# Layer 0's prologue in a new order: block 0's x loaded second, constants on two queues, the statistics of the other blocks inside block 0, the attention weight products spread out

## The reference, cut to what matters

```
xn = layernorm(x)
x  = x + mamba_block(xn) + moe(xn)          # layer 0
xn = layernorm(x)
x  = x + latent_attention(xn) + top2_moe(xn) # layer 1

mamba_block(x): r = rmsnorm(x) * rms_w
    xi, z = split(r @ in_proj)               # 256 + 256
    xi = silu(causal_conv4(xi) + conv_b)
    dt, B, C = split(xi @ x_proj)            # 8 + 16 + 16
    delta = softplus(dt @ dt_w + dt_b);  A = -exp(A_log)
    h = exp(delta*A) * h + (delta*xi)*B      # a scan over 256 tokens, 256 x 16 states
    return x + ((h . C) + xi*D) * silu(z) @ out_proj
moe(x): softmax over 8 experts, top-p 0.8 gate, 8 experts 128 -> 512 -> 128 with relu
```

## Time and profile before

| | |
|---|---|
| device time, median of 3 runs | 2266.21 us (2262.88 to 2268.63) |
| the profiled execution: device time, span | 2265.14 us, 2263.3 us |
| busy in the span | PE 1996.5 us (88%), DVE 1732.8 (77%), ACT 1335.6 (59%), POOL 1288.6 (57%) |
| granted TensorE clock, mean | 0.942 |
| layer 0's prologue (to the first scan) | 100.64 us |
| layer 0 / layer 1 boundary | near 1480 us |

### The profile page before, as it was taken

The page is one execution under the profiler, slowest core; times in us unless marked ns, Lnnn a source line. Parts: engine busy times, 40 slices in busy tenths (PEclk is TensorE's granted clock), DMA queues, the critical chain, the costliest instruction groups (busy, mean ns, idle before and its releaser), DMA issues. The chain is left out here.

```text
span 2263.3 us, 40460 instructions
## 1 busy us (share of the span) xinstructions
PE 1996.5 (88%) x13648; PEld 1155.7 (51%) x13714; DVE 1732.8 (77%) x2781; ACT 1335.6 (59%) x2421; POOL 1288.6 (57%) x972
## 2 busy tenths in 40 slices
PE   1799999999999999999999999945899999998885
PEld 0455555555555555555555555533455555544442
DVE  3498888888888889888888888854777777765544
ACT  1576776776776776766767767611355555544442
POOL 0477867767767767767768777623322222224540
PEclk9999999999999999999999999955899999998987
DMA  7514505415325335335145055041222222233437
GB/s 192 136 41 107 130 27 127 112 39 128 97 51 132 86 67 132 76 77 132 53 99 131 30 118 122 15 123 63 83 92 87 88 88 88 88 112 102 141 94 227
DMA packets 197004, 222.49 MB, mean 98 GB/s; under 512 B 28872, under 2 KB 139504, under 8 KB 192688
## 3 DMA queue, kind: packets, MB, share of 16 engines
q1 hardware_dynamic: 194736, 215.52, 37.0%
q0 software_dynamic: 2048, 4.18, 0.7%
HBM read 165.41 MB, written 54.27 MB: 97 GB/s over the span
## 5 line engine op out<-in xcount | busy, mean ns | idle before, releaser
L685 POOL TENSOR_TENSOR dBx<-REP,BC 128x1024 f32<-128x1024 f32 x256 | 603.0, 2358 | 288.2 <-DVE dA L845 243.2
L845 DVE TENSOR_TENSOR_SCAN dA<-dA,dBx 128x512 f32<-128x512 f32 x512 | 626.6, 1224 | 115.1 <-ACT dA L555 66.2
L374 PE MATMUL UP<-xnT,W 128*128 128x512 f32 x1024 | 518.4, 626 | 52.0 <-ACT hT L564 40.1
L383 PEld LDWEIGHTS DN<-W,hT 128*128 128x128 f32 x4096 | 469.4, 192 | 109.3 <-issue 97.6
L383 PE MATMUL DN<-W,hT 128*128 128x128 f32 x4096 | 496.0, 278 | 0.3 <-ACT GD L571 0.3
L564 ACT ACTIVATE hT<-UP,b 128x512 f32<-128x512 f32 x512 | 355.1, 694 | 88.7 <-PE UP L374 85.0
L555 ACT ACTIVATE dA<-REP,A 128x512 f32<-128x512 f32 x512 | 354.1, 695 | 72.4 <-DVE PR L854 72.1
L854 DVE TENSOR_TENSOR PR<-dA,BC 128x512 f32<-128x512 f32 x512 | 353.6, 691 | 31.5 <-DVE dA L845 18.8
L1705 DVE TENSOR_REDUCE NM<-S 128x4 f32<-128x1024 f32 (+1 forms) x192 | 234.5, 1221 | 148.5 <-PE S L1264 93.5
L374 PEld LDWEIGHTS UP<-xnT,W 128*128 128x128 f32 x1024 | 180.6, 195 | 278.5 <-issue 146.2
L1466 ACT ACTIVATE PT<-S 128x1024 f32<-128x1024 f32 x192 | 196.4, 1023 | 181.5 <-PE S L1278 135.2
(11 more groups left out here) (246 smaller groups left out, 2809.6 us busy)
## 6 DMA issues: line engine op xcount, KB each, us to landing
REP<-s_delta SPq DMA_DIRECT2D x128, 256.0 KB, 7.8
REP<-s_dx SPq DMA_DIRECT2D x128, 256.0 KB, 7.3
BC<-s_b SPq DMA_DIRECT2D x128, 256.0 KB, 8.7
s_parts<-SPL SPq DMA_DIRECT2D x32, 384.0 KB, 2.8
s_dx<-tz SPq DMA_DIRECT2D x16, 512.0 KB, 3.1
s_y<-zeros SPq DMA_DIRECT2D x32, 256.0 KB, 4.8
WE<-in_L_ffn_we SPq DMA_DIRECT2D x32, 256.0 KB, 4.5
YC<-s_y SPq DMA_DIRECT2D x16, 512.0 KB, 4.9
```

Source lines behind the costliest of these rows:

```text
L374: nc.tensor.matmul(UP[k % 2][:], W1[:, e % E0, f * P:(f + 1) * P], xnT[:, q, :], start=True, stop=True).then_inc(upf.sem, 1)
L383: last = nc.tensor.matmul(DN[:, j * P:(j + 1) * P], hT[:, e % 2, f, j * P:(j + 1) * P], W2[:, e, f, :], start=(f == 0), stop=(f == FB - 1))
L685: nc.gpsimd.tensor_tensor(dBx[:, s % 2], DX[:, h, j:j + 2, :], BC[:, q // 2, q % 2, :].unsqueeze(1).to_broadcast([P, 2, T0]), ALU.mult).th ...
L845: nc.vector.tensor_tensor_scan(h, h, dBx[:, k // 2 % 2, k % 2, :], 0.0, ALU.mult, ALU.add).then_inc(scan_done.sem, 1)
```

## The change

The first load takes eight tiles, the tiles of blocks 0 and 1, and their `norms` run at once (`FIRST` = 8 tiles, `OTHERS` = 56, in 7 DMAs of 8). SP then loads `XI` of block 0, five constants (`first_loads`, semaphore `needed`), ten constants (A_log, `xproj`; semaphore `loaded`), `dloads`, the other tiles of x, `wloads`, `forget`, b2. ACT issues the nine other constants itself. `prep` hangs on `needed` alone; scaling `outproj` and A moves to s = 4 (`prep2`). The `norms` of the other tiles are cut in three parts that run on DVE in slots 8, 12 and 15 of block 0, with their square roots on ACT in slots 9 and 13; the first user is now block 2. The weight products stand at s = 0, 2, 8, 9, 12. `start()` on all engines moves from h = 31 to h = 27. `BC<-s_b` of the first half (4 DMAs) goes out right after the store of B and C.

```diff
-    XC, XT = 6, (NT - J0) // 6
+    XC, XT = 7, (NT - 2 * J0) // 7
...
-    FIRST, OTHERS = slice(0, J0), slice(J0, NT)
-    STATS_END = 2 * XC
-    PROJ0 = 8
+    FIRST, OTHERS = slice(0, 2 * J0), slice(2 * J0, NT)
+    STATS_AT = {2: (0,), 4: (1,), 5: (2,), 6: (3,), 7: (4,), 8: (5, 6)}
+    LAST_STATS = 8
+    NORMS_AT, ROOTS_AT = (8, 12, 15), (9, 13)
+    PE_PROJ = {0: ((0, 0),), 2: ((0, 1), (1, 0)), 8: ((1, 1),), 9: ((2, 0),), 12: ((2, 1),)}
+    ACT_PROJ = {1: ((0, 0),), 3: ((0, 1),), 4: ((1, 0),), 9: ((1, 1), (2, 0)), 13: ((2, 1),)}
+    PREP_AT = 4
+    START_AT = 27
...
+            if h == START_AT:
+                start()
             if h >= HS - EARLY:
                 fore(h - HS, 1, 1)
-        start()
...
             if h == -EARLY and start:
                 load_x(0)
+                for dst, src in first_loads:
+                    sp.dma_start(dst, src, allow_slow_non_contiguous=True).then_inc(needed, 16)
+                for dst, src in loads[:10]:
+                    sp.dma_start(dst, src, allow_slow_non_contiguous=True).then_inc(loaded, 16)
+                sp.wait_ge(zeroed, 1)
+                for dst, src in dloads:
+                    sp.dma_start(dst, src, allow_slow_non_contiguous=True).then_inc(dloaded, 16)
+                for g in range(XC):
+                    tiles = slice(2 * J0 + g * XT, 2 * J0 + (g + 1) * XT)
+                    sp.dma_start(X0[:, tiles, :], xd[:, tiles, :]).then_inc(xloaded[g + 1], 16)
                 for dst, src in wloads:
                     sp.dma_start(dst, src, allow_slow_non_contiguous=True).then_inc(wloaded, 16)
-                for dst, src in dloads:
-                    sp.dma_start(dst, src, allow_slow_non_contiguous=True).then_inc(dloaded, 16)
+                for par in range(2):
+                    for k in range(HALF):
+                        sp.dma_start(seqs(d_d[par][k * P:(k + 1) * P, :])[:, :, 0:1], forget[:].unsqueeze(2), allow_slow_non_contiguous=True).then_inc(forgot, 16)
...
                 if start:
                     load_x(1)
+                    load_states(0, n, q)
...
-        pe.wait_ge(loaded, LOADED)
+        pe.wait_ge(needed, NEEDED)
         pe.wait_ge(prep, 1)
...
         def start():
+            pe.wait_ge(prep2, 1)
             pe.wait_ge(wloaded, 16 * (len(wloads) + J0))
...
+        for dst, src in loads[10:]:
+            act.dma_start(dst, src, allow_slow_non_contiguous=True).then_inc(loaded, 16)
...
+            if first and h in ROOTS_AT:
+                root(OTHERS, ROOTS_AT.index(h), stat_step2, root_done2)
...
-                if isinstance(n, int) and n == 1:
+                if isinstance(n, int) and n == 2:
                     pool.wait_ge(stat_step2, 21)
...
+            if first and h in NORMS_AT:
+                norms(OTHERS, NORMS_AT.index(h), stat_step2, root_done2)
```

More of the change, by code:

```diff
@@ L243, in _ @@
         xd = tokens(dram["L0_attn_x"].rearrange("b t d -> (b t) d"))
[L244 to L253, removed]
-                sp.dma_start(seqs(d_d[q][k * P:(k + 1) * P, :])[:, :, 0:1], forget[:].unsqueeze(2), allow_slow_non_contiguous=True).then_inc(forgot, 16)
         for s in (xi_loaded, b_stored, d_stored, e_stored, *bc_loaded, *dr_loaded, *dx_loaded, xo_stored):
             sp.sem_inc(s.sem, 2 * s.per)
+        sp.dma_start(X0[:, FIRST, :], xd[:, FIRST, :]).then_inc(xloaded[0], 16)
         def load_rep(rep, src, h, loaded):
@@ L334, in fore @@
                 load_dx(0, n, q)
-            elif h == SP_AT["bc0"]:
+            elif h == SP_AT["bc0"] and not start:
                 load_states(0, n, q)
@@ L452, in fore @@
             if h == PE_AT["xproj"]:
+                if isinstance(n, int) and n == 0:
+                    pe.wait_ge(loaded, LOADED)
                 pe.wait_ge(xi_done.sem, xi_done.at(n, 1))
@@ L495, in between @@
         def between(s):
-            if PROJ0 <= s < PROJ0 + 6:
-                project((s - PROJ0) // 2, (s - PROJ0) % 2)
+            for n, part in PE_PROJ.get(s, ()):
+                project(n, part)
         def end(it, par):
@@ L509, in _, with root @@
             act.sem_inc(s.sem, 2 * s.per)
-        def roots(tiles, stat_step, root_done):
-            act.wait_ge(stat_step, 7)
-            nc.scalar.activation(stats[:, tiles, 0], q1[:, tiles], ACT.Sqrt).then_inc(root_done, 1)
-            act.wait_ge(stat_step, 15)
-            nc.scalar.activation(stats[:, tiles, 0], q2[:, tiles], ACT.Sqrt).then_inc(root_done, 1)
-        roots(FIRST, stat_step, root_done)
-        act.wait_ge(loaded, LOADED)
-        nc.scalar.activation(A[:], A[:], ACT.Exp).then_inc(aexp, 1)
+        def root(tiles, part, stat_step, root_done):
+            act.wait_ge(stat_step, (7, 15)[part])
+            nc.scalar.activation(stats[:, tiles, 0], (q1, q2)[part][:, tiles], ACT.Sqrt).then_inc(root_done, 1)
+        for dst, src in loads[10:]:
+            act.dma_start(dst, src, allow_slow_non_contiguous=True).then_inc(loaded, 16)
+        for part in range(2):
+            root(FIRST, part, stat_step, root_done)
+        act.wait_ge(needed, NEEDED)
         act.wait_ge(prep, 1)
@@ L539, in between @@
         def between(s):
-            if PROJ0 <= s < PROJ0 + 6:
-                project((s - PROJ0) // 2, (s - PROJ0) % 2)
-            if s == STATS_END:
-                roots(OTHERS, stat_step2, root_done2)
+            for n, part in ACT_PROJ.get(s, ()):
+                project(n, part)
+            if s == PREP_AT:
+                act.wait_ge(loaded, LOADED)
+                nc.scalar.activation(A[:], A[:], ACT.Exp).then_inc(aexp, 1)
         LAST_IN_BANK = {0: -1, 1: 0, 2: -2}
@@ L577, in start @@
             act.wait_ge(wTc, 6)
+            act.wait_ge(prep2, 1)
             make_da(TILES, -1)
@@ L766, in fore @@
                 tri = tri8[:].rearrange("p (e o) -> p e o", o=E0).unsqueeze(1).to_broadcast([P, J0, E0, E0])
+                if isinstance(n, int) and n == 0:
+                    pool.wait_ge(loaded, LOADED)
                 pool.wait_ge(gate_step.sem, gate_step.at(n, 7))
@@ L820, in between @@
                     last = nc.vector.bn_stats(stats[:, i, :], X0[:, i, :])
-                if s == STATS_END - 1:
-                    last.then_inc(stat_step2, 1)
-            elif s == STATS_END:
-                norms(OTHERS, stat_step2, root_done2)
-            elif s == SLOTS - 1:
+            if s == LAST_STATS:
+                last.then_inc(stat_step2, 1)
+            if s == PREP_AT:
+                dve.wait_ge(loaded, LOADED)
+                nc.vector.tensor_scalar(outproj[:], outproj[:], 0.5, None, ALU.mult)
+                dve.wait_ge(aexp, 1)
+                nc.vector.tensor_scalar(A[:], A[:], -1.0, SLOWEST, ALU.mult, ALU.min).then_inc(prep2, 1)
```

80 lines of the change are left out of this document (42 added, 38 removed).

## The result

| | before | changed |
|---|---|---|
| device time, median of 20 runs each | 2267.95 us | 2257.07 us |
| ratio | | 0.9949 (95% interval 0.9938 to 0.9960) |
| span of the profiled execution | 2263.3 us | 2251.9 us |
| first scan | 100.64 us | 79.40 us |
| first scan of block 1 | 184.24 us | 169.52 us |

The kernel became 10.9 us faster by the medians, 11.6 by the ratio. Forecast was 19; 2257.07 lies 1 us above the range. The direction and its cause are as forecast, the size is a little over half.

A forecast was written before the change was run, and what follows sets the result against it. PE and DVE are nearly full from the first scan on, so a us off the prologue is a us of the kernel. First scan 24.8 us earlier, less 6.0 for norms, is -18.8: 2246.3, 2247 by the median, range 2239 to 2256.

The forecast's parts named there:

- Loads that come first, first weight product, rest of the front: Front of block 0: matmul of 41.91 starts at 26.7, 15.2 us earlier; POOL's delta near 54.4, 16.1 us earlier.
- What the second queue is worth: Prologue: nine constants issued by ACT leave SP's list, saving 9 x 0.46 = 4.1 us on the path.
- SP's list behind `dloads`: End of prologue: delta stored 1.3 us late, loaded back at 62.0; first scan at 75.8, 24.8 us earlier.
- PE at the same place: Start of block 1's work on PE: x0 at 79 to 80, 21 to 22 us earlier.
- `norms` in block 0: Block 0: the moved norms cost DVE 6.0 us, all charged; their two roots cost ACT's path 0.
- No change from block 1 on: Expected sign: block 0 some 4 to 6 us longer, and no change in the blocks behind it.
- D: Rival: prologue's gain lost later or smaller, as PE's early start meets a half clock; 2260 to 2266, chance 0.03.
- C: Rival: more gained in block 0, DVE's idle time takes 2 to 4 us of norms, forget not held; 2239 to 2242, 0.11.
- Rival A: Rival: in the prologue SP's list waits longer ahead of forget, 5 to 8 us more; 2252 to 2255, chance 0.15.
- B: Rival: block 0 pays twice for the norms, 6.0 us on DVE and 5.7 on ACT; 2253, chance 0.13.
- E: Rival: ACT's nine small DMAs hold SP's issues back equally, so dloads comes 4.1 us later; 2251, chance 0.03.
- F: Rival: slower, as PE's start waits for b2, the last piece of wloaded; 2274 with b2 at 90, chance 0.02.

The follow-up runs named there:

- one_queue: Changed kernel, but SP issues the nine constants that ACT issues, ahead of the weight pieces; ratio to before 0.9948.
- bc_after_dst: Changed kernel, but the four BC loads are issued behind the store of delta instead of ahead of it; ratio to before 0.9945.
- w2_late: Changed kernel, but W2 (2 MB of expert weights) is loaded behind the loads of delta and dx; ratio to before 0.9917.
- split: Changed kernel, but the transposes of the weight products wait for the three W_down alone, the products for the 18 small pieces; ratio to before 0.9942.
- pool_last: Changed kernel, but POOL's start (the first dBx) stands again behind h = 31, after XQ and XN of block 1; ratio to before 0.9919.
- pool_last_norms_tail: Changed kernel, but POOL's start stands behind h = 31 and the norms of the 56 other tiles run ahead of the first scan; ratio to before 0.9898.
- forget_act: Changed kernel, but ACT issues the four stores of forget at its start, behind its constants, instead of SP; ratio to before 0.9965.
- best2: Changed kernel with POOL's start, first exponentials and roots behind h = 31, norms ahead of first scan, transposes waiting for W_down alone, W2 behind dx; ratio to before 0.9899.

## Why the prediction was wrong

- *Loads that come first, first weight product, rest of the front*: right, mechanism and size (27.9 for 26.7; delta 53.6 for 54.4). The last small piece was issued 1.4 us later than summed, because the `xproj` loads took 4.68 us and not 3.43.
- *What the second queue is worth*, 4.1 us: its step measured 2.9 us at the front (one_queue), since the `xproj` loads took 1.3 us longer to issue (why is not shown), and 1.6 to 2.2 at the first scan. The rule of the Trainium skill, "DMA: Bandwidth & Descriptors", section "Issuing engines are not separate DMA queues", is that only the sequencer's time is saved, which is usually small. The traces agree on what was saved, and 2.9 us is not small here.
- *SP's list behind `dloads`*, the landing of delta's store ("now at 62.0"): the first step that failed, by 3.5 us, which the first scan has as 3.6 (79.4 for 75.8). The prediction allowed 4.0 us from the store of delta (58.0) to its load back (62.0), and they took 7.1 (58.33 to 65.48), of which SP waited 5.1 for the store. The next link, 11.3 us from there to the landing of dx, held (11.4). SP got to each store within 1 us of the forecast, in part by luck: the four `forget` stores took less than the 4.4 us given to them, and the hold ahead of them lasted longer. What was left out is that the stores and loads share one stream of bytes: BC's megabyte, which this change moves ahead of delta's store, had no price in the sum. bc_after_dst shows it: with BC behind the store, the load back came 4.3 us after it. It also shows that this order gives nothing in the end, since the megabyte then stands ahead of dx. w2_late shows that fewer bytes do help (4.6 to 5.2 us), and split that the front was not the path. A count of bytes comes out near the measured time: BC, the two stores, delta and dx are about 4.2 MB, at the 221 GB/s of the stretch 19 us, from 56.5 to 75.5, and dBx started at 76.9. It is an estimate, since the queue was not full all that time: the DMA share was 0.58 from 64 to 66 and 0.66 from 66 to 68, where SP waited for the store.
- *PE at the same place*, 21 to 22 us earlier: the second step that failed; measured 17.1 (83.92 against 100.99). 3.5 of the missing 4 to 5 came with the late dx. I wrote that PE would then be the one that waits for DVE, and so gave the handover no price. It was the other way round: x0 of block 1 stood 0.35 us behind the first scan before, and 4.5 us behind it now. The handover costs 2.7 us (pool_last), since XQ stands behind the first dBx on POOL. The prediction saw that order and did not ask who was ahead.
- *`norms` in block 0*, 6.0 us on the path: block 0 did become 6.5 us longer, which looks like a hit and is luck. Removing the norms alone gives back 2.9. The three pieces kept DVE for 7.0 us, not 6.0 (1.4 of it are two multiplies that were stopped while POOL was at work, see below), but in the kernel before DVE had 4.5 us idle in that part of block 0. "DVE is 95% busy there" was read from the first 40 us of block 0, and the `norms` stand 24 to 45 us behind the first scan. The 6.5 us are norms and handover together (6.8 in pool_last_norms_tail). On ACT, which I costed at nothing, the two roots stand in a stretch that is now 36.25 of 40 us full. A table load took 1.28 us there and the root began 0.02 us behind it each time. The Trainium skill, "ScalarE: Activation LUTs", section "What ACT_TABLE_LOAD costs", has 1380 ns of drain on top for every switch. The traces don't show such a drain, and the measurement decides.
- *No change from block 1 on*: holds within scatter; 1.5 us in all may be there.
- *The rivals.* The granted clock (D) fell from 0.98 to 0.96 over block 0, and no run has its price apart. The row that D took for the slow clock, 2.07 us at 41.91, stands where the profile gives the granted clock as 1.00 (40 to 45), so it doesn't show that price either. C was right in that DVE's idle time took some of the `norms`, and the handover took that gain away again. B, E and F did not come.

Added up: 24.8 - 3.6 = 21.2 at the first scan, less 6.5 in block 0 is 14.7 at block 1, and 11.4 at the end of the profiled pair. Of the 18.8 forecast, 3.6 are the stream, 0.5 block 0, and 3.3 lie between block 1 and the end in this pair of traces. Over two traces of each kernel block 1 starts 14.1 us earlier, and the ratio says 11.6: some 2 to 3 us of the miss stay unplaced, and more if the second measurement of the changed kernel (0.9973) is the better one. A part is scatter in the row the forecast started from: over two traces of each kernel the first scan is 20.5 us earlier, not 21.2. Rival A (late list) was the nearest in mechanism, and its place was wrong: SP reached the stores when forecast, and the bytes were late.

## What to carry to other kernels

In a prologue, add up the bytes that the queue still has to move ahead of the load that releases the first real work, over all stores and loads in their order; issue times being right say little when the queue is full. When a start is pulled forward, ask of each engine in turn what it stands behind, since an engine that was released earlier than its partner waits for it, and the gain is nearer that of the later one. Read how full an engine is in the very stretch where the new work will stand, and not in the one beside it. And put deferred work into idle time ahead of a wait that exists anyway: here DVE was idle for 16 us, and took 7 us of statistics into a nearly full block instead.

## What the runs showed of the hardware that was not expected

- An issue behind some 4 MB of loads held SP for about 10 us, whatever it was: 10.55 us for the one load of `Wq_down` before, 12.44 for the four stores of `forget` (one of them 10.4), 11.2 for the four loads of b2 (forget_act), 11.3 for the four of BC (w2_late, one of them 9.9). Where of the expert weights W1 alone stood ahead (w2_late), the four `forget` stores took 3.1 us and none was held. The hold costs what stands behind it in the list, not the DMA that is held.
- DMAs spread back over partitions ran at 221 GB/s (66 to 76 in the changed kernel), plain loads of x at 345.
- Two DVE multiplies of small SBUF tensors stopped while POOL was at work. In best2's timeline a multiply of 56 columns that took 0.26 us elsewhere took 1.55 and 2.27, each until one of POOL's two dBx (2.3 us each) was over:

```profile
69.29 4.64 POOL L708 TENSOR_TENSOR dBx<-REP,BC 128x1024 f32<-128x1024 f32 x2 [7.07 <-DMA REP<-s_dx]
```

```profile
70.19 1.55 DVE L1042 TENSOR_TENSOR stats<-rrms 128x56 f32<-128x56 f32 x1
71.78 2.27 DVE L1044 TENSOR_TENSOR stats<-stats,q 128x56 f32<-128x56 f32 x1
74.08 0.22 DVE L1046 TENSOR_SCALAR stats<-stats 128x56 f32<-128x56 f32 x1
```

The two multiplies lost 3.3 us, and without that best2's first scan could have stood at about 71.5 instead of 74.8 (an estimate from these rows). The same happened in block 0 of the changed kernel, where the same multiply took 1.38 us, until POOL's dBx was over:

```profile
121.31 2.35 POOL L702 TENSOR_TENSOR dBx<-REP,BC 128x1024 f32<-128x1024 f32 x1
```

```profile
122.40 1.38 DVE L1037 TENSOR_TENSOR stats<-rrms 128x56 f32<-128x56 f32 x1
```

The Trainium skill, "SBUF — State Buffer", section "Terms", describes a port pair shared by these two engines on which the loser blocks for a whole instruction. The rows agree.
